# Row-sum reciprocals moved from VectorE to GpSimd in a mixed attention kernel

## The chip, the core and the metric

The kernel runs on one core of one Trainium2 chip. The metric is the device time of one execution in microseconds. The engines are named as in the profile: PE is TensorE's matmul, PEld its weight load, DVE is VectorE, ACT is ScalarE, POOL is GpSimd and SP is SyncE with the DMA queue.

## What is computed

The reference runs four stages on 2 x 1024 tokens of width 128, each added to its input: a Mamba block, a mixture of 8 experts, a stack of six attention layers and a feed-forward stage with 4-bit quantisation. The change lies in the attention layers, and there in the softmax over each head's scores, whose weights are averaged over 16 heads:

```
q = (h @ wq.T + bq_).reshape(bh, sl, H, DH)      # H = 16 heads, DH = 8
k = (h @ wk.T + bk_).reshape(bh, sl, H, DH)
scores = jnp.einsum('blhd,bmhd->bhlm', q, k) * inv_sqrt_d
w_avg = jax.nn.softmax(scores, axis=-1).mean(axis=1)
new_w = jax.nn.softmax(CSCALE * w_avg + rel[None], axis=-1)
sa = jnp.einsum('blm,bme->ble', new_w, h)
h1 = _ln(h + sa, l1w, l1b)
h2 = _ln(h1, l2w, l2b)
ff = jax.nn.relu(h2 @ w1.T + b1_) @ w2.T + b2_
return (_ln(h2 + ff, l3w, l3b), None)
```

## The kernel before

Every engine has a program of its own, written as a loop in a fixed order; semaphores tie the engines together. The attention stage is one loop of 839 steps q that each engine walks. A piece x is 32 queries with 4 heads, a tile of 128 rows (4 heads x 32 queries) by 1024 keys, and a step handles two pieces. There are 1536 pieces. Four pieces (16 heads of the same 32 queries) are a quad, of which there are 384. Two quads are a block (64 queries, 192 blocks), two blocks a tile of 128 queries, and four tiles (512 queries, 16 quads) a half. Six layers, two sequences and two halves each make 24 halves.

For a piece, PE makes the scores in one of three PSUM buffers (`scores`, L696), DVE takes the negative row maximum into NM (`rowmax`, L1275), and ACT takes the exponential into one of nine E buffers and the row sum into a column of ZS (`soft`, L960). When the four sums of a quad are there, their reciprocals RZ are made, and from them a diagonal of weights `dg` (L1517, on POOL). PE then multiplies with `dg` as the loaded weights, which divides by the row sums and adds up the heads in one go (`weigh`, L707). The order on PE inside a step is

```
if 2 * q + 3 < N:
    scores(2 * q + 3)
...
if old:
    weigh(2 * q - 6)
if 2 * q + 4 < N:
    scores(2 * q + 4)
```

so the weighing of a quad's first piece stands three steps behind its scores, and all that PE does later waits behind it. `soft(x)` needs `weigh(x - 9)` to be done, because E has nine buffers.

After a block, ACT evacuates the averaged weights with an exponential (`evac`, L922, into acc), POOL multiplies them with the factor of the relative position (`rel0 rel1`, L1458), DVE transposes them in blocks of 32 (`turn`, L1216, into ET), and PE applies them to the tokens (`attend`, L640). DVE adds the residual (L1223) and takes the row statistics (L1228).

After a half follow the layer norms, the feed-forward part and the projection for the next layer. They are cut in small parts, and tables (`BLOCK_DUE`, `TILE_DUE`, `HALF_DUE`) say at which step and place of an engine each part stands. POOL has in them the variance (`pv`, L1436 to L1446), the power of -0.5 that makes the reciprocal root (`pw`, L1451 and L1453), the norms (`ln`, L1468 to L1474, which write ZA, HB and the next H), `hb` (L1478) and the splitting of the projected tile into three bf16 parts (`sp`, 16 operations L1490 to L1496 on UB). PE transposes the finished HB (`h2t`, L645), and ACT copies the result to hT (L925). POOL's place of the diagonal is the head of every second step:

```
for q in range(STEPS):
    if 0 <= q - 1 < PAIRS and q % 2 == 0:
        diag(q // 2 - 1)
    for n, p in due("POOL", q, "d"):
        post_pool(e, n, p)
```

On DVE the reciprocal stands between the two row maxima of the same steps. POOL doesn't wait for anything but semaphores, and its operations run strictly in the order of the program.

Of the kernel before, what the change touches and what calls it, by code (L numbers as in the profile page):

```python
# [7 lines left out]
ALU = mybir.AluOpType  # L8
# [133 lines left out]
PAIRS = BLOCKS * 4  # L142
# [51 lines left out]
def last(engine, step, place):  # L194

    return LAST[engine].get((step - 1 - PAIRS, place), "").split()
# [19 lines left out]
def due(engine, step, place):  # L216

    out = []
    step -= 1
    for half in range(max(-2, step // 32 - 3), min(HALF_N, step // 32 + 1)):  # L220
        for p in HALF_DUE[engine].get((step - 32 * half - 31, place), "").split():
            if p[:2] in ("pj", "sp"):
                if half < HALF_N - 4:
                    out.append((half, p))
            elif p == "fin":
                if half >= HALF_N - 4:
                    out.append((half, p))
            elif half >= 0:
                out.append((half, p))
    for tile in range(max(0, step // 8 - 2), min(TILES, step // 8 + 1)):  # L230
        for p in TILE_DUE[engine].get((step - 8 * tile - 7, place), "").split():
            out.append((tile, p))
    for block in range(max(0, step // 4 - 2), min(BLOCKS, step // 4 + 1)):
        for p in BLOCK_DUE[engine].get((step - 4 * block - 3, place), "").split():
            out.append((block, p))
    return out
# [46 lines left out]
def build(nc, io):  # L283
    ctx = ExitStack()
    with ctx:
        s = Sems(nc, ctx)
        V, A_, G, PE_ = nc.vector, nc.scalar, nc.gpsimd, nc.tensor

        def sbuf(c, name, shape, dt=F32):
            return c.enter_context(nc.sbuf_tensor(name, shape, dt))  # L290
# [67 lines left out]
        mask = sbuf(pn, "mask", [128, 32])  # L358
# [26 lines left out]
        pt = ExitStack()  # L385
# [7 lines left out]
        dg = sbuf(pt, "dg", [128, 3, 4, 32])  # L393
        NM = sbuf(pt, "NM", [128, 4])
        ZS = sbuf(pt, "ZS", [128, 3, 4])
        RZ = sbuf(pt, "RZ", [128, 3, 4])
        st = sbuf(pt, "st", [128, 2, 3, 4, 6])
        smp = sbuf(pt, "smp", [128, 2, 3, 4, 4])
# [553 lines left out]
        def attention_act(e):  # L952
            def soft(x):
# [4 lines left out]
                if quad >= 3 and j == 0:  # L958
                    e.wait_ge(s["rz"], quad - 2)
                A_.activation(E[:, x % NE, :], bank[x % 3][:, :], ACT.Exp, bias=NM[:, x % 4:x % 4 + 1],  # L960
                              accum_out=ZS[:, quad % 3, j:j + 1]).then_inc(s["exp"], 1)

# [247 lines left out]
        def post_dve(e, n, p):  # L1210
            if p == "turn":
                tile, j = divmod(n, 2)
                e.wait_ge(s["rel"], 2 * n + 2)
                if tile and j == 0:
                    e.wait_ge(s["attend"], 4 * tile)
                V.transpose(ET[:, :, 64 * j:64 * j + 64].rearrange("p i (g q) -> p g i q", g=2),  # L1216
                            acc[:, n % 2, :].rearrange("p (g i q) -> p g i q", g=2, i=8)).then_inc(s["turn"], 1)
            elif p == "add1":
                o, a, r = pb(7), n // 4 % 2, n % 4
                e.wait_ge(s["attend"], 4 * n + 4)  # L1220
                V.reciprocal(rz2[:, n % 2:n % 2 + 1], o[:, 128:129]).then_inc(s["rz2"], 1)
                e.wait_ge(s["rz2"], n + 1)
                V.scalar_tensor_tensor(ZA[:, a, r, :], o[:, 0:128], rz2[:, n % 2:n % 2 + 1], H[:, n // 8 % 3, n % 8, 0:128],  # L1223
                                       ALU.mult, ALU.add).then_inc(s["add1"], 1)
            elif p == "bn0":
                a, r = n // 4 % 2, n % 4
                e.wait_ge(s["add1"], n + 1)
                V.bn_stats(st[:, a, 0, r, :], ZA[:, a, r, :]).then_inc(s["tbn0"], 1)  # L1228
            elif p == "add2":
                e.wait_ge(s["ff2"], 8 * n + 8)  # L1230
                e.wait_ge(s["h2b"], 4 * n + 4)
                V.tensor_tensor(HB[:, :, :], pb(7).rearrange("p (n d) -> p n d", n=4), ZA[:, n % 2, :, :], ALU.add).then_inc(s["add2"], 1)
            else:
                k, a, t = int(p[2]), n % 2, int(p[3])
                src = (ZA[:, a], ZA[:, a], HB)[k]
                if k == 1:
                    e.wait_ge(s["tln"], 12 * n + 1 + t)
                elif t == 0:
                    e.wait_ge(s["add2"], n + 1)
                V.bn_stats(st[:, a, k, t, :], src[:, t, :]).then_inc(s["tbn"], 1)  # L1240
# [27 lines left out]
        def attention_dve(e, own):  # L1268
            def rowmax(x):
                if x >= N:  # L1270
                    return
                e.wait_ge(s["scores"], x + 1)
                if x >= 4:
                    e.wait_ge(s["exp"], x - 3)
                V.tensor_reduce(NM[:, x % 4:x % 4 + 1], bank[x % 3][:, :], AX.X, ALU.max, negate=True).then_inc(s["rowmax"], 1)  # L1275

            rowmax(0)
            for q in range(STEPS):
                rowmax(2 * q + 1)
                if 0 <= q - 1 < PAIRS and q % 2 == 0:  # L1280
                    quad = q // 2 - 1
                    e.wait_ge(s["exp"], 4 * quad + 4)
                    if quad >= 3:
                        e.wait_ge(s["diag"], quad - 2)
                    V.reciprocal(RZ[:, quad % 3, :], ZS[:, quad % 3, :]).then_inc(s["rz"], 1)  # L1285
                for n, p in due("DVE", q, "m"):
                    post_dve(e, n, p)
                rowmax(2 * q + 2)
                for p in last("DVE", q, "m"):
                    ffn_dve(e, own, p)  # L1290
                for n, p in due("DVE", q, "e"):
                    post_dve(e, n, p)
                for p in last("DVE", q, "e"):
                    ffn_dve(e, own, p)
# [212 lines left out]
                            sc.unsqueeze(2).to_broadcast([128, n, 16]), ALU.mult).then_inc(done, 1)  # L1507

        def attention_pool(e, own):
            e.wait_ge(s["mask"], 4)  # L1510
            e.wait_ge(s["ld_rel"], 16)

            def diag(quad):
                e.wait_ge(s["rz"], quad + 1)
                if quad >= 3:
                    e.wait_ge(s["weigh"], 4 * quad - 8)
                G.tensor_tensor(dg[:, quad % 3, :, :], mask[:, :].unsqueeze(1).to_broadcast([128, 4, 32]),  # L1517
                                RZ[:, quad % 3, :].unsqueeze(2).to_broadcast([128, 4, 32]), ALU.mult).then_inc(s["diag"], 1)
# [6 lines that stand above are left out]
                for p in last("POOL", q, "d"):  # L1525
                    ffn_pool(e, own, p)
                for n, p in due("POOL", q, "f"):
                    post_pool(e, n, p)
                for p in last("POOL", q, "f"):
                    ffn_pool(e, own, p)  # L1530

        def ffn_pool(e, own, p):
            j = int(p[2])
            w = slice(4 * j, 4 * j + 4)
            if p == "wr0":
                requant_pool(e, s["fp4_cut"], 1, WQ0[0], WQ0[2], WQ0[3], WQ0[4], own, s["fp4w"])
            elif p == "wr1":
                requant_pool(e, s["fp4_cut"], 2, WQ1[0], WQ1[2], WQ1[3], WQ1[4], own, s["fp4w"])
            elif p[:2] == "pr":
                e.wait_ge(s["ln_bn"], 10 * j + 10)  # L1540
                own.then(G.tensor_tensor(lrs[:, w], lva[:, w], mhalf[:, 0:4], ALU.pow))
                G.tensor_tensor(lnb[:, w], lnm[:, w], lrs[:, w], ALU.mult).then_inc(s["ln_nb"], 1)
            elif p[:2] == "rq":
                u = QUANT[f"qt{j}"]
                requant_pool(e, s["cut"], u + 1, XQ[:, w, :].rearrange("p n d -> p (n d)"),
                             QA[:, u % 2, 0:4 * D], QP[:, u % 2, 0:4 * D], QC[:, u % 2, 0, 0:32], own, s["requant"])
            else:
                u = QUANT[f"qh{j}"]
                if j >= 2:
                    e.wait_ge(s["ht"], GT * (j - 2) + GT)  # L1550
                requant_pool(e, s["cut"], u + 1, HQ[:, j % 2, :, :].rearrange("p n d -> p (n d)"),
                             QA[:, u % 2, :], QP[:, u % 2, :], QC[:, u % 2, 0, 0:GT * NBL], own, s["requant"])
# [179 lines left out]
```

## Time and profile before

| What | Before |
|---|---|
| Median of 3 runs | 2952.5 us (2948.83 to 2958.75) |
| The profiled execution | 2956.46 us, span 2954.7 us |
| Mean granted TensorE clock | 0.976 |
| PE busy | 2588.4 us (88%) |
| DVE busy | 2539.2 us (86%) |
| ACT busy | 2359.0 us (80%) |
| POOL busy | 1292.7 us (44%) |
| First and last reciprocal | 633.5 and 2828.3 us |

The attention stage is the time from about 625 to 2865 us. A busy share is a mean over stages and doesn't say by itself which engine sets the pace in one of them; the idle time of an engine that nobody waits for costs nothing.

### The profile page before, as it was taken

How to read it: one execution, taken by the hardware profiler on the slowest of the kernel's cores; microseconds unless marked ns; L12 is line 12 of the kernel's file. 1: busy time of each engine (PE TensorE's matmuls, PEld its weight loads, DVE VectorE, ACT ScalarE, POOL GpSimd, SP SyncE). 2: the span in 40 equal slices, each digit the busy share in tenths (PEclk: the TensorE clock that was granted, in tenths of full speed). 3: DMA queues.
4: the chain of work that ended last, by engine and by line, in shares of the span. 5: the costliest groups of instructions: out<-in, count | busy, mean ns of one | idle time of the engine just before them, and what ended most of it. 6: DMA issues, size and time to landing. Idle time of an engine off the chain costs nothing.

```text
span 2954.7 us, 79002 instructions
## 1 busy us (share of the span) xinstructions
PE 2588.4 (88%) x31053; PEld 1430.0 (48%) x31053; DVE 2539.2 (86%) x3677; ACT 2359.0 (80%) x4175; POOL 1292.7 (44%) x2668
## 2 busy tenths in 40 slices
PE   6888899978998998988889889998898888999856
PEld 3444476744444444544445444454444444444435
DVE  4888836389999999999899899998999899999966
ACT  5778543459999898998899889898898898988842
POOL 2101122122556544565345554456544566444564
PEclk8999999989999999999999999999999999999988
DMA  2000000412222123131231312312123121220000
GB/s 63 1 1 1 16 1 12 59 46 45 39 34 43 27 38 56 32 45 32 31 60 29 45 29 34 59 31 42 30 32 59 29 45 29 34 44 10 2 1 15
DMA packets 86770, 94.44 MB, mean 32 GB/s; under 512 B 4592, under 2 KB 84736, under 8 KB 85632
## 3 DMA queue, kind: packets, MB, share of 16 engines
q1 hardware_dynamic: 86400, 89.41, 19.3%
q8 instruction: 245, 4.01, 0.6%
q14 instruction: 125, 1.02, 0.1%
HBM read 69.47 MB, written 19.92 MB: 30 GB/s over the span
## 4 chain that ended last, share of the span: by engine, by line
PE 51%; issue 12%; DVE 11%; POOL 9%; ACT 7%; ACTq 0%; POOLq 0%; DVEq 0%
PE bank L707 15%; PE bank L696 13%; DVE NM L1275 6%; PE bank L640 6%; ACT E L960 4%; PE bank L622 4%; PE bank L612 3%; PE bank L659 3%; PE bank L652 2%; ACT acc L922 2%; POOL acc L1458 1%; PE bank L677 1%; DVE ET L1216 1%; POOL HB L1474 1%; POOL HB L1468 1%
## 5 line engine op out<-in xcount | busy, mean ns | idle before, releaser
L1275 DVE TENSOR_REDUCE NM<-bank 128x1 f32<-128x1024 f32 x1536 | 1811.4, 1212 | 142.6 <-PE bank L696 130.5
L960 ACT ACTIVATE E<-bank,NM 128x1024 f32<-128x1024 f32 x1536 | 1708.9, 1115 | 238.2 <-DVE NM L1275 153.8
L707 PE MATMUL bank<-E,dg 128*32 128x256 f32 x12288 | 970.1, 385 | 106.0 <-ACT acc L922 97.9
L696 PE MATMUL bank<-KS,QS 128*32 128x512 bf16 x12288 | 965.0, 383 | 93.4 <-ACT E L960 70.7
L707 PEld LDWEIGHTS bank<-E,dg 128*32 128x32 f32 x12288 | 356.0, 109 | 423.7 <-issue 229.7
L696 PEld LDWEIGHTS bank<-KS,QS 128*32 128x32 bf16 x12288 | 328.2, 96 | 480.0 <-ACT E L960 289.1
L1458 POOL TENSOR_TENSOR acc<-acc,rel 128x256 f32<-128x256 f32 x384 | 273.3, 733 | 380.2 <-ACT acc L922 380.2
L1517 POOL TENSOR_TENSOR dg<-mask,RZ 128x128 f32<-128x128 f32 x384 | 153.6, 400 | 564.0 <-DVE RZ L1285 564.0
L960 ACT ACTIVATION_READ_ACCUMULATOR E<-bank,NM 128x1 f32 x1536 | 304.6, 198 | 0.0
L640 PE MATMUL bank<-H,ET 128*128 128x129 f32 x1536 | 224.3, 288 | 7.4 <-issue 4.4
L640 PEld LDWEIGHTS bank<-H,ET 128*128 128x128 f32 x1536 | 187.1, 191 | 89.3 <-issue 79.5
L1204 DVE SCALAR_TENSOR_TENSOR EO<-bank,OH,EO 128x128 f32<-128x128 f32 x256 | 72.0, 344 | 132.2 <-PE bank L622 132.0
L908 ACT ACTIVATE HS<-bank,cst 128x512 f32<-128x512 f32 x128 | 87.3, 686 | 112.4 <-PE bank L612 112.3
L549 PE MATMUL bank<-hC,ident 128*128 128x512 f32 x256 | 144.6, 649 | 8.4 <-DVE XS L1054 7.1
L622 PEld LDWEIGHTS bank<-W,HS 128*128 128x128 f32 x1024 | 124.2, 192 | 30.4 <-issue 29.6
L1216 DVE STREAM_TRANSPOSE ET<-acc 128x512 f32<-128x512 f32 x192 | 134.7, 702 | 4.0 <-POOL acc L1458 3.9
L863 ACT ACTIVATE dBT<-UT,BT 128x256 f32<-128x256 f32 x256 | 108.6, 496 | 24.5 <-PE bank L533 24.1
L622 PE MATMUL bank<-W,HS 128*128 128x128 f32 x1024 | 124.6, 275 | 0.0
L922 ACT ACTIVATE acc<-bank 128x512 f32<-128x512 f32 x192 | 113.7, 592 | 10.5 <-PE bank L707 9.0
L612 PE MATMUL bank<-RTr,W 128*128 128x512 f32 x256 | 121.5, 597 | 0.1
L659 PEld LDWEIGHTS bank<-WL,UB 128*128 128x128 f32 x768 | 94.5, 191 | 50.7 <-issue 48.2
L659 PE MATMUL bank<-WL,UB 128*128 128x128 f32 x768 | 116.6, 291 | 1.9 <-ACT UB L933 1.8
(228 smaller groups left out, 2712.5 us busy)
## 6 DMA issues: line engine op xcount, KB each, us to landing
KS<-scratch SPq DMA_DIRECT2D x216, 128.0 KB
QS<-scratch SPq DMA_DIRECT2D x216, 128.0 KB
scratch<-UB SPq DMA_DIRECT2D x24, 768.0 KB, 3.8
WL<-in_wl SPq DMA_DIRECT2D x6, 1091.0 KB, 19.4
X<-in_x SPq DMA_DIRECT2D x4, 256.0 KB, 6.3
W<-in_moe_w SPq DMA_DIRECT2D x1, 1024.0 KB, 8.6
out<-X SPq DMA_DIRECT2D x8, 128.0 KB, 1.8
rel<-in_rel SPq DMA_DIRECT2D x1, 960.0 KB, 5.0
```

The source lines that it names most:

```text
L612: PE_.matmul(pb(2 * (n % 2) + hc), W1[:, ex, hc * 128:hc * 128 + 128], RTr[:, toks(j)], start=True, stop=True).then_inc(s["moe_up"], 1)
L622: inst = PE_.matmul(pb(4 + q % 2)[:, t * 128:t * 128 + 128], HS[:, q % 3, hc, t * 128:t * 128 + 128], W2[:, ex, hc, :], start=(hc == 0), s ...
L640: inst = PE_.matmul(o[:, 0:129], ET[:, i, :], H[:, n // 8 % 3, i, :], start=(i == 0), stop=(i == 7))
L659: inst = PE_.matmul(o[:, t * 128:t * 128 + 128], fT[:, fc, t * 128:t * 128 + 128], wl(l, "w2", fc * 128, 128), start=(fc == 0), stop=(fc = ...
L696: inst = PE_.matmul(bank[x % 3][32 * i:32 * i + 32, k * 512:k * 512 + 512], QS[:, half % 2, 4 * hq + i, r0:r0 + 32], KS[:, b, 4 * hq + i, ...
L707: inst = PE_.matmul(pb(6)[32 * k:32 * k + 32, 256 * grp:256 * grp + 256], dg[:, x // 4 % 3, x % 4, :], E[:, x % NE, :].rearrange("p (i k c ...
L922: A_.activation(acc[:, n % 2, :], pb(6), ACT.Exp, scale=1.0 / NHEAD).then_inc(s["evac"], 1)
L960: A_.activation(E[:, x % NE, :], bank[x % 3][:, :], ACT.Exp, bias=NM[:, x % 4:x % 4 + 1], accum_out=ZS[:, quad % 3, j:j + 1]).then_inc(s[" ...
L1216: V.transpose(ET[:, :, 64 * j:64 * j + 64].rearrange("p i (g q) -> p g i q", g=2), acc[:, n % 2, :].rearrange("p (g i q) -> p g i q", g=2, ...
L1275: V.tensor_reduce(NM[:, x % 4:x % 4 + 1], bank[x % 3][:, :], AX.X, ALU.max, negate=True).then_inc(s["rowmax"], 1)
L1458: G.tensor_tensor(y, y, rel_of(n % 16 * 64 + 32 * grp), ALU.mult).then_inc(s["rel"], 1)
L1517: G.tensor_tensor(dg[:, quad % 3, :, :], mask[:, :].unsqueeze(1).to_broadcast([128, 4, 32]), RZ[:, quad % 3, :].unsqueeze(2).to_broadcast( ...
```

## The change

The reciprocals of ZS leave DVE. POOL makes them at the head of `diag`, as a power: a tile `mone` of 128x4 holds -1.0 and is filled once at the start of attention. The waits that DVE had (for the fourth exponential of the quad, and for the diagonal three quads back) go to POOL, and the diagonal now waits for POOL's own result.

```
+        mone = sbuf(pt, "mone", [128, 4])
...
                 rowmax(2 * q + 1)
-                if 0 <= q - 1 < PAIRS and q % 2 == 0:
-                    quad = q // 2 - 1
-                    e.wait_ge(s["exp"], 4 * quad + 4)
-                    if quad >= 3:
-                        e.wait_ge(s["diag"], quad - 2)
-                    V.reciprocal(RZ[:, quad % 3, :], ZS[:, quad % 3, :]).then_inc(s["rz"], 1)
                 for n, p in due("DVE", q, "m"):
...
         def attention_pool(e, own):
-            e.wait_ge(s["mask"], 4)
+            G.memset(mone[:, :], -1.0).then_inc(s["mask"], 1)
+            e.wait_ge(s["mask"], 5)
             e.wait_ge(s["ld_rel"], 16)
 
             def diag(quad):
+                e.wait_ge(s["exp"], 4 * quad + 4)
+                if quad >= 3:
+                    e.wait_ge(s["diag"], quad - 2)
+                G.tensor_tensor(RZ[:, quad % 3, :], ZS[:, quad % 3, :], mone[:, :], ALU.pow).then_inc(s["rz"], 1)
                 e.wait_ge(s["rz"], quad + 1)
                 if quad >= 3:
                     e.wait_ge(s["weigh"], 4 * quad - 8)
```

The line numbers of the changed kernel differ: PE's, ACT's and most of DVE's are one higher, POOL's parts of the norms five lower, and `dg` stays L1517. The order of instructions on POOL behind the row statistics of a half, before the change:

```order
L1458 TENSOR_TENSOR acc<-acc,rel 128x256 [waits s_evac] x2
L1517 TENSOR_TENSOR dg<-mask,RZ 128x128 [waits s_weigh,s_rz]
L1494 TENSOR_SCALAR UB<-UB 128x2x128 [waits s_split] x2
L1436 TENSOR_TENSOR smp<-st 128x4 [waits s_tbn]
L1437 TENSOR_TENSOR smp<-st 128x4
L1438 TENSOR_TENSOR smp<-st 128x4
L1440 TENSOR_TENSOR smp<-smp 128x4 [waits s_tvar]
L1441 TENSOR_SCALAR smp<-smp 128x4
L1442 TENSOR_SCALAR smp<-smp 128x4
```

The same place on POOL in the changed kernel, where the third diagonal of that part of the program stands:

```order
L1453 TENSOR_TENSOR acc<-acc,rel 128x256 [waits s_evac] x2
L1513 TENSOR_TENSOR RZ<-ZS,mone 128x4 [waits s_diag,s_exp]
L1517 TENSOR_TENSOR dg<-mask,RZ 128x128 [waits s_weigh,s_rz]
L1489 TENSOR_SCALAR UB<-UB 128x2x128 [waits s_split] x2
L1431 TENSOR_TENSOR smp<-st 128x4 [waits s_tbn]
L1432 TENSOR_TENSOR smp<-st 128x4
L1433 TENSOR_TENSOR smp<-st 128x4
L1435 TENSOR_TENSOR smp<-smp 128x4 [waits s_tvar]
L1436 TENSOR_SCALAR smp<-smp 128x4
L1437 TENSOR_SCALAR smp<-smp 128x4
```

One row has come in, the power, between the products with the relative position and the diagonal; it stands so ahead of every diagonal. On DVE, the same part of the program before (`turn` is L1216, the row maxima L1275):

```order
L1285 RECIPROCAL RZ<-ZS 128x4 [waits s_diag,s_exp]
L1240 BN_STATS st<-ZA 128x6 [waits s_tln] x2
L1275 TENSOR_REDUCE NM<-bank 128x1 [waits s_exp,s_scores] x2
L1216 STREAM_TRANSPOSE ET<-acc 128x2x8x32 [waits s_rel]
L1275 TENSOR_REDUCE NM<-bank 128x1 [waits s_exp,s_scores] x2
L1285 RECIPROCAL RZ<-ZS 128x4 [waits s_diag,s_exp]
L1275 TENSOR_REDUCE NM<-bank 128x1 [waits s_exp,s_scores] x2
```

And in the changed kernel:

```order
L1241 BN_STATS st<-ZA 128x6 [waits s_tln] x2
L1276 TENSOR_REDUCE NM<-bank 128x1 [waits s_exp,s_scores] x2
L1217 STREAM_TRANSPOSE ET<-acc 128x2x8x32 [waits s_rel]
L1276 TENSOR_REDUCE NM<-bank 128x1 [waits s_exp,s_scores] x4
L1222 RECIPROCAL rz<-bank 128x1 [waits s_attend]
```

The two reciprocals are gone and nothing else has moved on DVE.

## Rows read from the trace of the kernel before

**Rows 1.** The page, the chain that ended last: shares of the span by engine.

```profile
PE 51%; issue 12%; DVE 11%; POOL 9%; ACT 7%; ACTq 0%; POOLq 0%; DVEq 0%
```

**Rows 2.** Waits: who waited for whom, us in total, times, longest us.

```profile
POOL dg L1517 <- DVE RZ L1285: 564.0, 129, 10.1
...
PE bank L645 <- POOL HB L1474: 18.7, 22, 1.2
```

**Rows 3.** Busy time by stretch: us, then each engine's, clock, DMA share, GB/s.

```profile
1557.16:1587.19 30.03, 26.09 (x388) 13.09 (x380) 28.97 (x37) 27.78 (x50) 28.48 (x64) 1.00 0.09 29
1587.19:1647.94 60.75, 56.44 (x795) 30.63 (x799) 56.31 (x74) 54.78 (x97) 19.80 (x43) 1.00 0.33 41
```

**Rows 4.** Timeline, 1557 to 1589 us: start us, us, engine, line [idle before <-releaser].

```profile
1557.16 0.21 POOL L1436 TENSOR_TENSOR smp<-st 128x4 f32<-128x4 f32 x1 [0.78 <-DVE st L1228]
...
1560.31 0.40 POOL L1517 TENSOR_TENSOR dg<-mask,RZ 128x128 f32<-128x128 f32 x1
1560.67 1.03 POOL L1451 TENSOR_TENSOR smp<-smp,mhalf 128x4 f32<-128x4 f32 x1
1561.77 0.20 POOL L1453 TENSOR_TENSOR smp<-smp 128x4 f32<-128x4 f32 x1
...
1566.30 0.40 POOL L1517 TENSOR_TENSOR dg<-mask,RZ 128x128 f32<-128x128 f32 x1
...
1586.47 0.72 POOL L1474 TENSOR_TENSOR HB<-HB,WL 128x256 f32<-128x256 f32 x1
...
1587.34 0.63 PE L645 MATMUL bank<-ident,HB 128*128 128x128 f32 x4 [0.79 <-POOL HB L1474]
...
1588.64 0.59 ACT L925 ACTIVATE hT<-bank 128x512 f32<-128x512 f32 x1
```

**Rows 5.** Timeline of PE: the first and the last of 21 such transposes.

```profile
763.24 0.63 PE L645 MATMUL bank<-ident,HB 128*128 128x128 f32 x4 [0.88 <-POOL HB L1474]
...
2602.01 0.63 PE L645 MATMUL bank<-ident,HB 128*128 128x128 f32 x4 [0.82 <-POOL HB L1474]
```

**Rows 6.** Groups by line and shape: busy us, mean ns | idle before.

```profile
L1285 DVE RECIPROCAL RZ<-ZS 128x4 f32<-128x4 f32 x384 | 63.3, 165 | 0.8 <-ACT E L960 0.8
...
L1517 POOL TENSOR_TENSOR dg<-mask,RZ 128x128 f32<-128x128 f32 x384 | 153.6, 400 | 564.0 <-DVE RZ L1285 564.0
L1451 POOL TENSOR_TENSOR smp<-smp,mhalf 128x4 f32<-128x4 f32 x72 | 73.7, 1024 | 0.4
...
L1345 POOL TENSOR_TENSOR xrs<-xva,mhalf 128x8 f32<-128x8 f32 x4 | 6.6, 1642 | 13.5 <-DVE xva L1026 13.5
```

**Rows 7.** Timeline of DVE at one reciprocal.

```profile
1564.91 0.17 DVE L1285 RECIPROCAL RZ<-ZS 128x4 f32<-128x4 f32 x1
1564.99 1.20 DVE L1275 TENSOR_REDUCE NM<-bank 128x1 f32<-128x1024 f32 x1
```

**Rows 8.** Timeline, POOL, DVE and PE's weight loads, 1572 to 1586 us.

```profile
1572.75 0.40 POOL L1517 TENSOR_TENSOR dg<-mask,RZ 128x128 f32<-128x128 f32 x1
1573.48 0.70 DVE L1216 STREAM_TRANSPOSE ET<-acc 128x512 f32<-128x512 f32 x1
1573.95 0.34 PEld L707 LDWEIGHTS bank<-E,dg 128*32 128x32 f32 x8
...
1578.88 0.40 POOL L1517 TENSOR_TENSOR dg<-mask,RZ 128x128 f32<-128x128 f32 x1
...
1584.26 0.40 POOL L1517 TENSOR_TENSOR dg<-mask,RZ 128x128 f32<-128x128 f32 x1
...
1584.56 0.70 DVE L1216 STREAM_TRANSPOSE ET<-acc 128x512 f32<-128x512 f32 x1
...
1585.04 0.34 PEld L707 LDWEIGHTS bank<-E,dg 128*32 128x32 f32 x8
```

**Rows 9.** PE's timeline after a pause, and the stretch behind it.

```profile
1456.04 0.40 PE L707 MATMUL bank<-E,dg 128*32 128x256 f32 x1 [3.15 <-issue]
...
1456.40:1459.80 3.40, 3.40 (x40) 1.51 (x32) 2.02 (x2) 2.41 (x4) 0.11 (x1) 0.51 0.24 31
```

## The prediction

> **What bounds the kernel now.** I read the page's chain first. It shows 51% of the span on PE and 12% on issue, against 11% on DVE and 9% on POOL [rows 1]. So the reciprocal's own engine carries a tenth of the path, and the engine that gets the reciprocal is nearly as much on it, although it is busy only 44% of the span. That made me ask where POOL is late. The two waits say it [rows 2]. POOL sits idle for 564.0 us waiting for the reciprocal, so on the whole it has room. But PE waits 22 times, 18.7 us together, for the normalised tile HB that POOL makes. A half (512 queries of one layer) transposes HB once, so this is a wait of nearly each of the 24 halves.
>
> The stretches of one half show the same [rows 3]. From 1557.16 to 1587.19 us POOL is busy 28.48 of 30.03 us; in the 60.75 us behind it POOL is busy only 19.80 us, while PE is busy 56.44. The POOL timeline of the first stretch is one unbroken string [rows 4]: it starts when the last row statistics of the half are there (L1436) and ends with HB (L1474, ended at 1587.19), and the missing 1.55 us are gaps of 0.1 us behind POOL's own results. PE's transpose starts 0.15 us later, after 0.79 us of idleness. The same wait stands in 21 halves, the first at 763.24 and the last at 2602.01 us [rows 5]. I call these 30 us the string. In the string POOL is the bound; in the rest of a half it is PE with ACT and DVE close behind.
>
> **The change, step by step.** *Removed from DVE:* 384 reciprocals, 165 ns each, 63.3 us busy [rows 6]. They don't cost that much time: one starts at 1564.91 and the row maximum behind it at 1564.99 [rows 7], so it takes 0.08 us of DVE's time, since it overlaps its neighbours. All of them come to 384 x 0.08 = 31 us of DVE time. Outside the strings there are 384 - 21 x 5 = 279 of them, 22 us, and only where DVE sets the pace, which by the chain [rows 1] is a small part. I take 6 us; the bounds are 0 and 31.
>
> *Added to POOL:* 384 powers of a 128x4 tile. The trace has this operation 72 times with the exponent -0.5, 1024 ns each (and 1642 ns for 128x8) [rows 6]. The power is followed by the diagonal, which waits for it. What such a pair costs stands in the string: the power L1451 starts at 1560.67 and L1453, which waits for it, at 1561.77 [rows 4]. So each power puts 1.10 us in front of its diagonal. The exponent -1 is not in the trace; the lower bound is a plain 128x4 operation (0.20 us, L1453 [rows 4]) with the same 0.08 us behind it, 0.28 us, the upper one the 128x8 power, 1.72 us. I take 1.10, because shape, engine and operation are the same.
>
> *What hides a power:* outside the strings POOL's idle time. There the power can start as soon as the last of four exponentials has ended, and no longer after DVE's next row maximum, so the diagonal comes about when it came before. In the string there is no cover. Five diagonals lie in it, at 1560.31, 1566.30, 1572.75, 1578.88 and 1584.26 [rows 4, 8]; the order shows a power ahead of each, and the sixth diagonal lies behind HB. So HB comes 5 x 1.10 = 5.5 us later, and PE, which waits for it already, transposes 5.5 us later.
>
> *Where the 5.5 us first show:* earlier in the string, at two diagonals. The third ends at 1573.15, and PE loads its weights at 1573.95 [rows 8]: 0.80 us of slack against three powers, 3.3 us, so PE stalls 2.5 us. The fifth ends at 1584.66 with PE at 1585.04: 0.38 us of slack, plus the 2.5 us by which PE is already behind, against 5.5 us, so it stalls another 2.6 us. The rest, 0.4 us, is waited for at HB. On the way DVE's block transpose waits as well: at 1573.48, where its input is ready at 1572.79 (where the diagonal starts), two powers make it 1.5 us late; at 1584.56 four powers make it 1.6 us late. Neither is added: they run beside PE's stalls. Queued behind PE's stalled load are the scores of the next head groups, so row maxima and exponentials stop too, within about one piece of 1024.
>
> *What comes back:* at the transpose the other engines stand a little ahead of where they stood. ACT copies the transposed tile at 1588.64 although PE has finished it at 1587.97 [rows 4]; at most these 0.67 us are saved. I take 0.5 us, which leaves 5.0 us for a half.
>
> *The halves at the end:* halves 22 and 23 have no projection of the next layer (16 POOL operations on UB fall away) and so have room in the string; I take 1 us each. Half 24 has no diagonals in it. Everything before attention gets one memset and is unchanged.
>
> The sum: 21 x 5.0 + 2 - 6 = +101 us. The profiled execution took 2956.5 us, 1.8 us outside its span, so 3057.5 us; it lay 4.0 us above the median of the three runs, 2952.5, and from that median the forecast is 3053.5 us, rounded to 3054.
>
> The Trainium skill (GPSIMD Engine Reference, Engine selection) speaks against such a move in general: two-input elementwise work on GpSimd takes about twice as long as on VectorE. Twice 0.165 is 0.33 us, an estimate from that page, where the trace has 1.02 us for a power; the page's ratio would give five insertions of 0.41 us, 2.05 us for a half. The trace disagrees with it for this operation, and I go by the trace.
>
> **The rivals.**
> *A cheaper power.* If the exponent -1 is a short path on POOL, an insertion could be near 0.4 us, between the 0.28 and the 1.10 above. Then the string grows by 2.0 us, a half by 1.5, and the sum is 21 x 1.5 + 1 - 6 = +27 us, 2980 us. For it speaks only that no row has this exponent; against it, that a power costs 0.8 us more than a plain operation of the same shape, 1.02 against 0.20 us [rows 4], which looks like the way powers are computed and not like a property of one exponent. (By the Trainium skill, GPSIMD Engine Reference, Engine selection, this is the case to expect.)
> *Faster than before.* DVE's share is real and all of it comes back, 31 us, while the string is filled with cheap powers. This decides if 21 x (5 x insertion - 0.5) is under 31, that is if an insertion is under 0.40 us; at the lower bound of 0.28 it is 21 x 0.9 - 31 = -12 us, 2940 us. The small chain share of DVE and every row of a power speak against it.
> *TensorE's clock falls in the stalls.* After PE was idle 3.15 us and started again at 1456.04, the granted clock was at its lower level (1.2 GHz, 0.51 on average) for 3.4 us, in which PE was busy all the time [rows 9]. The new stalls, 2.5 and 2.6 us, are nearly as long. The first is followed by POOL-bound time, where it costs nothing; the second lies just ahead of the transpose, so a low stretch would reach beyond it and cost up to half of 3.4 us, 1.7 us. In all halves that is 21 x 1.7 = 36 us more, 3090 us. Against it: PE's pauses here are cut by single operations, which the pause at 1456 was only in part.
> *The stalls add up.* DVE's two late transposes (3.1 us) come on top of PE's instead of beside them, by way of the attend step that needs them. Then POOL's string has waits in it that I counted as none: 21 x 8.1 + 2 - 6 = +166 us, 3119 us. Against it: POOL shows no wait for another engine inside the string now, and every power pushes it further behind what it might wait for.
> *No change*, because the waits of POOL [rows 2] swallow it all: only if the strings aren't strings, and 21 waits for HB of some 0.9 us say they are.
>
> **How the numbers follow.** A difference of 0.3% (9 us) is about what a measurement of this kernel tells from none. Forecast (3035 to 3078, an insertion within 0.2 us of 1.10): 0.62. Clock: 0.12. Cheaper power: 0.09. Stalls add up: 0.06. Faster: 0.06. No change: 0.05. The low end leaves out the cheaper power and what lies below it, the high end the adding stalls: 3005 to 3095. By sign: faster 0.06, same 0.05, slower 0.89.
>
> **What would show it.** In the changed profile: a POOL group with the power, x384, mean 1.02 us, 393 us in all, and POOL busy near 1690 us; the same string 35.5 us long with unbroken POOL; a new wait of PE's weight load for the diagonal, two per half and some 5 us together, 100 us in all; DVE's block transpose waiting for POOL's product some 3 us a half; the stretch behind HB still near 60 us long. Wrong would be: a power much shorter or longer than 1.02 us, a string much longer than 35.5 us, or a granted clock under 1 in each string.

## The result and the profile after

The changed kernel took 3078.95 us (median of 4 runs, 3072.26 to 3081.19) against 2954.61 us before: a ratio of 1.0413, with a 95% interval of 1.0387 to 1.0439, so +124 us. The prediction was 3054 us in a range of 3005 to 3095. The profiled execution of the changed kernel took 3072.26 us with a span of 3070.4, which is 115.7 us more than the span before.

The chain of the changed kernel, as shares of the span, against 9% for POOL and 11% for DVE before [rows 1]:

```profile
PE 45%; POOL 21%; issue 10%; DVE 9%; ACT 6%; POOLq 0%; ACTq 0%; DVEq 0%
```

POOL's busy share rose from 44% to 55% and is still the lowest of PE, DVE, ACT and POOL, but its share of the chain more than doubled. The powers, as a group of the page (busy us, mean ns | idle before):

```profile
L1513 POOL TENSOR_TENSOR RZ<-ZS,mone 128x4 f32<-128x4 f32 x384 | 388.5, 1012 | 211.6 <-ACT E L961 183.6
```

1012 ns is within 1.2% of what the power of -0.5 took (1024 ns) [rows 6], so the exponent makes next to no difference. The other operations kept their lengths (the diagonal 399 ns against 400, the products with the relative position 731 against 733, the row maxima 1214 against 1212), so moving the work made neither engine's other operations slower. The waits of the changed kernel (us in total, times, longest); before, the first two came to 0.5 and 3.9 us in all and the last to 18.7 [rows 2]:

```profile
PEld bank L708 <- POOL dg L1517: 98.8, 48, 2.7
...
DVE ET L1217 <- POOL acc L1453: 47.7, 41, 3.2
...
PE bank L646 <- POOL HB L1469: 31.9, 21, 1.6
```

PE's weight load now waits for the diagonal 48 times, a little over two for each of 21 halves. DVE's block transpose waits twice in a half, and the wait for HB has grown from 0.9 to 1.5 us. The half that begins at 1711.27 us shows them in order. The stretches of its string and of what is behind it, to be read against [rows 3]:

```profile
1711.27:1746.70 35.43, 27.62 (x388) 14.06 (x380) 30.23 (x33) 28.92 (x51) 33.49 (x69) 0.95 0.09 28
1746.70:1807.38 60.68, 56.32 (x794) 30.72 (x798) 54.27 (x62) 53.49 (x95) 30.82 (x52) 1.00 0.29 38
```

The string has grown from 30.03 to 35.43 us, and POOL is busy 33.49 of them. Behind it POOL took eleven more powers (19.80 to 30.82 us busy), and the stretch is not longer: 60.68 against 60.75 us. The timeline inside that string:

```profile
1729.08 0.71 DVE L1217 STREAM_TRANSPOSE ET<-acc 128x512 f32<-128x512 f32 x1 [1.52 <-POOL acc L1453]
...
1730.10 0.40 POOL L1517 TENSOR_TENSOR dg<-mask,RZ 128x128 f32<-128x128 f32 x1
...
1730.55 0.75 PE L708 MATMUL bank<-E,dg 128*32 128x256 f32 x8 [2.21 <-POOL dg L1517]
...
1743.77 0.40 POOL L1517 TENSOR_TENSOR dg<-mask,RZ 128x128 f32<-128x128 f32 x1
...
1744.22 0.64 PE L708 MATMUL bank<-E,dg 128*32 128x256 f32 x8 [1.08 <-POOL dg L1517]
...
1746.84 0.63 PE L646 MATMUL bank<-ident,HB 128*128 128x128 f32 x4 [1.55 <-POOL HB L1469]
...
1747.51 0.60 ACT L926 ACTIVATE hT<-bank 128x512 f32<-128x512 f32 x1 [0.57 <-PE bank L646]
...
1749.26 1.08 PE L653 MATMUL bank<-hT,WL 128*64 128x256 f32 x8
```

PE stalls at the third diagonal, at the fifth and at HB, in the places that the prediction named, and DVE's transpose is 1.52 us late ahead of the third.

TensorE's clock fell in 18 of the 21 strings, and at the end of the other three. This is the stretch behind the first stall of the half shown, with PE busy throughout and the granted clock at its lower level (1.2 GHz):

```profile
1730.90:1734.30 3.40, 3.40 (x28) 2.19 (x22) 2.36 (x3) 2.34 (x4) 3.07 (x12) 0.51 0.00 0
```

### The profile page after: what moved, and what is told of

Same layout as the page of the kernel before. It is cut to its first block, busy times and chain, and to the rows that moved or that the text cites. A ratio compares the mean times of both kernels' runs of the same rounds, so it can differ in the third digit from the quotient of the medians.

```text
span 3070.4 us, 79003 instructions
## 1 busy us (share of the span) xinstructions
PE 2632.1 (86%) x31053; PEld 1450.6 (47%) x31053; DVE 2518.2 (82%) x3293; ACT 2358.5 (77%) x4175; POOL 1678.9 (55%) x3053
## 4 chain that ended last, share of the span: by engine, by line
PE 45%; POOL 21%; issue 10%; DVE 9%; ACT 6%; POOLq 0%; ACTq 0%; DVEq 0%
PE bank L708 13%; PE bank L697 11%; PE bank L641 5%; DVE NM L1276 5%; PE bank L623 3%; ACT E L961 3%; PE bank L613 3%; POOL RZ L1513 3%; PE bank L660 3%; POOL acc L1453 3%; PE bank L653 2%; ACT acc L923 1%; POOL UB L1487 1%; POOL HB L1463 1%; POOL dg L1517 1%
## 5 line engine op out<-in xcount | busy, mean ns | idle before, releaser
L1276 DVE TENSOR_REDUCE NM<-bank 128x1 f32<-128x1024 f32 x1536 | 1801.2, 1214 | 233.7 <-PE bank L697 224.5
L1513 POOL TENSOR_TENSOR RZ<-ZS,mone 128x4 f32<-128x4 f32 x384 | 388.5, 1012 | 211.6 <-ACT E L961 183.6
L641 PEld LDWEIGHTS bank<-H,ET 128*128 128x128 f32 x1536 | 202.7, 205 | 93.1 <-issue 83.3
L641 PE MATMUL bank<-H,ET 128*128 128x129 f32 x1536 | 240.9, 303 | 6.1 <-issue 3.1
L1517 POOL TENSOR_TENSOR dg<-mask,RZ 128x128 f32<-128x128 f32 x384 | 153.2, 399 | 30.1
```

The source lines that it names most:

```text
L641: inst = PE_.matmul(o[:, 0:129], ET[:, i, :], H[:, n // 8 % 3, i, :], start=(i == 0), stop=(i == 7))
L1513: G.tensor_tensor(RZ[:, quad % 3, :], ZS[:, quad % 3, :], mone[:, :], ALU.pow).then_inc(s["rz"], 1)
```

## The experiments

Of each run the table gives the time, the ratio to executions of the kernel before that were taken beside it (their medians lie between 2953.3 and 2955.1 us), and two lengths that are read from the timeline in the way of [rows 4]: the string, from POOL's first variance operation of a half to the end of HB, as the mean of 21 halves; and what is behind it, from there to the next half's first variance operation, as the value of the undisturbed halves (single halves are longer, by pauses of PE and falls of its clock).

| Run | us (median) | ratio [95%] | string | behind |
|---|---|---|---|---|
| before | 2954.6 | 1 | 30.05 | 60.75 |
| changed | 3079.0 | 1.0413 [1.0387, 1.0439] | 35.44 | 60.69 |
| powers outside the strings alone | 2958.2 | 1.0001 [0.9983, 1.0020] | 30.04 | 60.68 |
| powers in the strings alone | 3082.4 | 1.0425 [1.0396, 1.0453] | 35.46 | 60.74 |
| no reciprocals at all | 2955.6 | 1.0005 [0.9988, 1.0023] | 30.06 | 60.68 |
| both operations | 3096.9 | 1.0478 [1.0454, 1.0502] | 35.45 | 61.02 |
| a product for the power | 2987.3 | 1.0120 [1.0098, 1.0143] | 31.52 | 60.69 |
| two powers | 3257.1 | 1.1029 [1.1009, 1.1049] | 40.99 | 63.3 |
| before, later transpose | 2956.6 | 1.0011 [0.9998, 1.0025] | 30.16 | 60.75 |
| powers outside, later transpose | 2956.4 | 1.0021 [1.0006, 1.0036] | 30.14 | 60.70 |
| changed, later transpose | 3059.1 | 1.0346 [1.0320, 1.0372] | 35.46 | 60.00 |
| no reciprocals, later transpose | 2955.0 | 1.0004 [0.9985, 1.0023] | 30.06 | 60.79 |

**1. Powers outside the strings, DVE's reciprocals inside.** The edit gives each quad to one of the engines, with a semaphore each:

```
def on_dve(quad):
    return quad >= 16 and quad % 16 in (3, 4, 5, 6, 7)
...
 attention_dve:
+    if 0 <= q - 1 < PAIRS and q % 2 == 0 and on_dve(q // 2 - 1):
+        ...
+        V.reciprocal(RZ[:, quad % 3, :], ZS[:, quad % 3, :]).then_inc(s["rzd"], 1)
 diag(quad):
+    if not on_dve(quad):
         ...
         G.tensor_tensor(RZ[:, quad % 3, :], ZS[:, quad % 3, :], mone[:, :], ALU.pow).then_inc(s["rz"], 1)
```

> The reciprocals of the five quads whose diagonals lie in each string (quads 3 to 7 of 16, from the second sixteen on, 115 in all) are made on DVE as before, the other 269 as powers on POOL. String theory: the string is 30.0 us again, PE doesn't wait for the diagonal, and the time is that of before or up to 9 us less (within 0.3%), since 269 powers in POOL's idle time cost nothing. Rival (every power costs its share, 124/384 = 0.32 us each): 269 x 0.32 = 87 us over before.

The ratio was 1.0001. 269 powers, 272 us of POOL's time, cost nothing that can be measured. PE's wait for HB is what it was before, and its weight load waits for the diagonal only once, 1.4 us, where the changed kernel has 48 such waits:

```profile
PE bank L656 <- POOL HB L1485: 18.2, 21, 0.9
```

**2. The mirror: powers inside the strings alone** (`on_dve` negated).

> The mirror of the run before: powers on POOL for those 115 quads, DVE's reciprocal for the other 269. String theory: the whole loss stays, string 35.4 us, 21 x 5.4 = +113 us over before and up to +128. Rival (each power its share): 115 x 0.32 = +37 us.

The whole loss came back: a ratio of 1.0425, while the 115 powers are only 117 us of POOL's time. Its waits are those of the changed kernel:

```profile
PEld bank L718 <- POOL dg L1534: 107.4, 52, 2.7
...
PE bank L656 <- POOL HB L1485: 32.6, 22, 1.6
```

The two runs together settle where the time went. A power costs nothing or about 1.1 us, by its place, and not the same share everywhere.

**3. No reciprocals at all.** RZ is a constant, set once; this leaves the division by the row sums out. The waits for RZ go with it.

```
 diag(quad):
-    G.tensor_tensor(RZ[:, quad % 3, :], ZS[:, quad % 3, :], mone[:, :], ALU.pow).then_inc(s["rz"], 1)
-    e.wait_ge(s["rz"], quad + 1)
```

> Leaves out the reciprocals: RZ is a constant that is set once, the diagonal waits for the fourth exponential alone. This is what taking the work off DVE is worth when nothing is added anywhere. String theory, in which DVE hardly sets the pace: before minus 0 to 12 us, string 30.0 us. Rival (DVE's 0.08 us each are on the path): minus 31 us; if the full 165 ns counted, minus 63 us.

The ratio was 1.0005. Behind the strings a half is 0.07 us shorter than before, which is 1.5 us in 21 halves. So the relief of DVE, which was the one thing on the change's credit side, is worth nothing that can be measured here: at most 3.5 us by the interval.

**4. The reciprocal on DVE and an unread power on POOL.**

```
 diag(quad):
     e.wait_ge(s["rz"], quad + 1)
+    G.tensor_tensor(pdm[:, quad % 3, :], RZ[:, quad % 3, :], mone[:, :], ALU.pow).then_inc(s["pdm"], 1)
+    e.wait_ge(s["pdm"], quad + 1)
```

> DVE makes the reciprocals as before, and POOL makes a power of RZ into a tile that nobody reads, ahead of the diagonal, which waits for it: POOL's cost without DVE's relief. String theory: the time of the changed kernel, within 10 us of 3079, string 35.4 us. Rival (DVE's relief is worth 31 us and the power costs more than the string shows): 3110 us.

The string was as long as in the changed kernel, but the time was 3096.9 us, 18 us over it and outside the 10 us that I had given. The stretch behind the string is 0.33 us longer (7 us in 21 halves): the last power of a half waits for DVE's reciprocal, so its diagonal ends about 1.2 us later, and POOL's work behind it then runs without a pause into the next string. The rest goes with falls of the clock that reached beyond the end of the string in 8 halves of the profiled execution, against 4 in the changed kernel's. Four of these 8 halves are 2.4 to 2.8 us longer behind the string than 61.02. Why the clock falls so late in more halves here stays open.

**5. A product for the power.** The reciprocal is left out; ZS is multiplied with a small constant.

```
-G.memset(mone[:, :], -1.0)
+G.memset(mone[:, :], 0.000001)
-G.tensor_tensor(RZ[...], ZS[...], mone[:, :], ALU.pow)
+G.tensor_tensor(RZ[...], ZS[...], mone[:, :], ALU.mult)
```

> In place of the power POOL multiplies ZS with a small constant (so the reciprocal is left out and the weights are wrong): the same place, waits and chain, but an operation of 0.2 us for one of 1.0 us. String theory: an insertion of 0.28 us, the string 30.0 + 5 x 0.28 = 31.4 us, 21 x 1.4 = +29 us over before, 2984 us. Rival (the cost is the wait of the diagonal for a result of POOL's own and the order, not the power's length): over 3040 us.

The time was 2987.3 us, 3 us from the forecast of the string theory. The string grew by 1.47 us for five insertions, 0.29 us each, with this operation:

```profile
L1513 POOL TENSOR_TENSOR RZ<-ZS,mone 128x4 f32<-128x4 f32 x384 | 78.5, 204 | 298.8 <-ACT E L961 244.8 <-PE bank L708 54.0
```

The insertion follows the operation's length: 0.29 us at 204 ns, 1.08 us (5.39 / 5) at 1012 ns. This excludes that the new wait or the order was what cost.

**6. Two powers ahead of each diagonal.**

```
+    G.tensor_tensor(pdm[:, quad % 3, :], RZ[:, quad % 3, :], mone[:, :], ALU.pow).then_inc(s["pdm"], 1)
+    e.wait_ge(s["pdm"], quad + 1)
```

> A second power ahead of each diagonal, of the first one's result, into a tile that nobody reads; the diagonal waits for it. String theory: 5 x 1.10 more in each string, 40.9 us, 21 x 5.4 = 113 us more than the changed kernel, 3192 us, and some 10 to 20 us on top from places outside the strings where the diagonal has 2.1 us of slack, as in the run with both operations: up to 3215 us. Rival (the string's other waits absorb it): under 3150 us.

The string was 40.99 us, as expected, but the time was 3257.1 us, 178 us over the changed kernel where I had 113 to 136. Strings account for 21 x 5.55 = 117 us, halves 22 and 23 for 10. Behind the strings a half was 2.6 us longer, 55 us in all. PE waits for diagonals three times as often as in the changed kernel:

```profile
PEld bank L709 <- POOL dg L1520: 278.9, 151, 4.4
```

Five of the seven waits of a half lie inside the string, though; the two behind it are 0.2 us each and can't make 2.6 us. Two other things do. The clock was at its lower level for 3 us or more behind the end of each of the 21 strings, as in this stretch, and DVE's first row maximum behind the string starts 3.1 us after HB instead of 1.8, so 1.3 us are lost there:

```profile
984.70:988.00 3.30, 3.15 (x28) 1.75 (x32) 0.15 (x1) 1.52 (x2) 3.14 (x6) 0.55 0.58 62
```

And at the end of a half POOL no longer waits for the row statistics with which the next string begins. In the changed kernel it did so for 0.85 us ahead of the string at 1711.27 and 26.6 us in all; here its last two diagonals have 2.2 us of powers more ahead of them, and only this is left (us, times, longest):

```profile
POOL smp L1432 <- DVE st L1230: 5.6, 4, 2.3
```

That delays the next string by another 2.2 - 0.85, about 1.3 us. I had expected 10 to 20 us outside the strings, from slack at the diagonals; neither of these two was in the sum.

**7. The kernel before with PE's transpose half a step later.**

```
-HALF_DUE = {"PE": {(17, "h"): "h2t", (18, "h"): "ff1_00 ff1_01", ...
+HALF_DUE = {"PE": {(18, "g"): "h2t", (18, "h"): "ff1_00 ff1_01", ...
```

> The kernel before with one entry of PE's table moved: the transpose of HB half a step later (from place h of step 17 to place g of step 18), so that PE does a weighing and a piece of scores first. If the string's end at HB sets the pace already in the kernel before, its 0.8 to 0.9 us of PE's idleness in 21 halves go: 10 to 18 us less, 2937 to 2945 us. Rival (ACT or DVE sets the pace there and PE's wait is idle time that costs nothing): 0 to 3 us less.

The rival was right: 1.0011, no gain. PE doesn't wait for HB any more, but the same place holds another wait of nearly the same length, in its timeline:

```profile
1501.32 0.61 PE L696 MATMUL bank<-KS,QS 128*32 128x512 bf16 x8 [0.68 <-ACT E L960]
1501.87 0.66 PE L645 MATMUL bank<-ident,HB 128*128 128x128 f32 x4
```

So before the change two bounds were level in the string: POOL's 30 us, and something that held PE's scores back for just as long. The wait says ACT's exponential, and with it the loop of scores, row maximum and exponential through three PSUM buffers; no run made a hop of that loop shorter, so this second bound is read from the wait and not shown.

**8. Powers outside the strings, with the later transpose.**

> The later transpose together with powers on POOL outside the strings and DVE's reciprocals inside (the first experiment). String theory: as the run with the later transpose alone or up to 5 us less, since DVE's relief outside the strings brought nothing. Rival (DVE becomes the bound once PE's wait is gone, so its relief counts): 10 us less or more than that.

The ratio was 1.0021, its interval just above 1: no better than either edit alone. None of the runs was faster than the kernel before.

**9. The changed kernel with the later transpose.**

> The changed kernel with PE's transpose of HB half a step later. In the kernel before, the same edit brought nothing, though PE had waited 0.9 us. If the reason is that another engine needed those 30 us of a half as well, and in the changed kernel POOL alone is late, then the edit must pay here: PE fills its wait of 1.55 us with a weighing and a piece of scores, 0.43 us each, 0.9 us in 21 halves, 18 us less than the changed kernel, about 3060 us. Rival (PE's wait for HB is never on the path): within 5 us of the changed kernel, 3074 to 3084 us.

The time was 3059.1 us, 20 us less than the changed kernel and 1 us from the forecast. The stretch behind the string is 0.69 us shorter, 14.5 us in 21 halves. In this profiled execution no fall of the clock reached from a string into it, which in the changed kernel had cost 1.3 us in each of 4 halves. The same edit that was worth nothing before is worth 20 us where POOL alone is late. PE's wait at HB shrank from 1.55 to 0.38 us:

```profile
1541.73 0.63 PE L646 MATMUL bank<-ident,HB 128*128 128x128 f32 x4 [0.38 <-POOL HB L1469]
```

**10. No reciprocals, with the later transpose** (the division is left out again).

> No reciprocals at all (left out, as in the third experiment) and the later transpose, so that POOL's string no longer holds PE at its end and DVE is relieved by 0.08 us five times in it. If DVE is the other engine that needs the 30 us: 21 x 0.3 to 0.4 us, 6 to 8 us less than before. If it is ACT or PE: no change.

The ratio was 1.0004, by the interval at most 4.4 us less than before, short of the 6 to 8 us that DVE as the bound would have given. So DVE, though busy 96% of the string [rows 3], isn't the second bound by its load. What is left is the round trip through PE, DVE and ACT, as the wait for ACT in run 7 suggests, or ACT's own load; which of them was not tried.

## Why the prediction was right

The measured 3079 us lie inside the stated range, but 1 us above the band (3035 to 3078) that was given 0.62 (by the sum, 0.2 us more or less for an insertion gives 3033 to 3075): the mechanism held, and two credits in the sum did not.

**The string as the bound: right, and shown.** Five insertions were forecast to lengthen it by 5.5 us to 35.5; it is 35.44 us in the mean of 21 halves, 5.39 more. Runs 1 and 2 put the whole loss in these halves' strings, and runs 5 and 6 give its slope on either side. 21 x 5.39 = 113 us.

**The price of a power: right.** 1.10 us for the pair was read from the root's power; it is 1.08. By the Trainium skill (Perfetto Trace Analysis, GPSIMD Engine Instruction) a GpSimd operation is better timed by the spacing of starts than by its reported span; the trace agrees, since a power lengthened the string by 1.08 us, which is nearer to the spacing (1.10) than to the span (1.01). By the Trainium skill (GPSIMD Engine Reference, Engine selection) an add, a product or a maximum of two inputs takes about twice as long on GpSimd as on VectorE. That ratio can't be carried over to this pair of a power and a reciprocal: 1012 against 165 ns is a factor of 6.1, and the measurement decides.

**Where the stalls show: right in place, their sizes only near.** Forecast were 2.5 us, 2.6 us and 0.4 us more at HB. The weight load waits up to 2.7 us at the third diagonal. In the half shown PE's matmuls stall 2.21 and 1.08 us, and 1.55 us at HB (0.8 more than before): the clock had fallen behind the first stall, and PE was later anyway. In the three halves in which the clock stayed up until the end of the string, the two stalls are 2.1 and 2.2 us, and one of 1.1 us at the fourth diagonal, which the prediction hadn't named, stands between them.

**What comes back: the term that was mis-sized.** I took 0.5 us per half, -10.5 us in all, because ACT could copy the transposed tile 0.67 us sooner. ACT did: its copy starts 0.67 us after the transpose (1747.51 against 1746.84), where it was 1.30 us behind it before [rows 4]. But the consumer, PE's first product with that tile, starts 2.42 us behind the transpose in both kernels: at 1749.26 after, and before in this row of the kernel before's timeline:

```profile
1589.76 1.08 PE L652 MATMUL bank<-hT,WL 128*64 128x256 f32 x8
```

Two weighings and two pieces of scores stand between on PE, so the earlier copy shortened nothing. Behind the string 0.06 us came back, 1 us in all.

**DVE's relief: mis-sized too.** I took -6 us; runs 1, 3 and 10 show none.

**The last halves: right.** 0.83 and 1.25 us for halves 22 and 23, where 1 each was taken.

In spans: 113 for the strings, 2 for halves 22 and 23, and 1 net for all else make the 115.7 us between the two profiled executions. That the rest comes to only 1 us is in part luck: falls of the clock cost some 5 us there, and pauses of PE that differ from one execution to the next took about as much back. With the sum's -10.5 and -6 taken out, the forecast of +101 would have been +117.5.

**The clock: a rival that came about without its price.** "A granted clock under 1 in each string" was among my signs of being wrong, and it came: 0.95 in the string shown. It was no sign against the mechanism. The clock fell for 3.4 us or more in or at the end of each of the 21 strings, but mostly behind the first stall, in time that POOL bounds. All 21 strings are 35.4 to 35.5 us long, with 0.2 us at the lower clock in them or 6.9. Only in 4 halves of the profiled execution did it reach from the end of the string into the stretch behind, and three of them, free of other pauses, are 62.0 us long there instead of 60.69: 1.3 us, close to the 1.7 that I had as a bound. One of the four shows it best: the transpose that took 0.63 us takes 1.09.

```profile
1649.41 1.09 PE L646 MATMUL bank<-ident,HB 128*128 128x128 f32 x4 [1.55 <-POOL HB L1469]
```

The medians lie 124 us apart and the profiled executions 116. The changed kernel's profiled run was the fastest of its four. More time at the lower clock doesn't explain the other three: their mean granted clocks, 0.962 and 0.963, are above the 0.960 of the profiled one. The cause of these 8 us stays open.

**The other rivals.** The cheaper power, the added stalls, the faster kernel and no change are excluded: by the group of the power, by the string's length, and by runs 1 to 3. With doubled powers (run 6) time is lost outside the strings too; what the trace shows there is the clock and POOL's own work, not DVE's late transposes.

## What to carry to other kernels

An engine with the lowest busy share can be the bound for a third of the time (here 30 of the 91 us of a half). Before moving work to it, find its unbroken strings, count how many of the moved operations fall into them, and price those alone; the others are free as long as the engine's idle time there lasts, and run 6 shows where it ends. A power on GpSimd takes as long as five plain small operations (1.01 against 0.20 us). A wait in front of an engine pays back only where no second bound is level with it: the same half step was worth nothing in one kernel and 20 us in the other.

## What the runs showed of the hardware

A GpSimd power of 128x4 takes 1.01 us for the exponents -0.5 and -1 alike, and a product of that shape 0.20 us. An operation on GpSimd that the next one waits for costs its span and 0.07 to 0.09 us more: 1.08 us for the power, 0.29 us for the product. DVE's reciprocal of that shape, 165 ns by its span, is worth at most 0.07 us a half when eleven of them are taken away behind a string.

Behind PE's stalls of 2.1 and 2.2 us the granted clock fell to 1.2 GHz for 3.4 us or more in each of the 21 halves of the changed kernel, though not always behind the first of them. A stall of that length doesn't always bring a fall: with the later transpose (run 9), stalls of 2.1 to 2.2, 1.1 and 2.2 us stood in 8 of the 21 strings without any. The string of one of them, with the clock at 1.00:

```profile
1019.98:1055.43 35.45, 27.11 (x404) 13.33 (x396) 30.13 (x33) 28.99 (x51) 33.51 (x69) 1.00 0.10 28
```
